# A tuned attention and expert block: value products in blocks of three score chunks, maximum pairs regrouped around them

## What is computed

```python
scores = jnp.einsum('bhqd,bhkd->bhqk', q, k) / jnp.sqrt(jnp.float32(Hd))
attn = jax.nn.softmax(scores, axis=-1)
out = jnp.einsum('bhqk,bhkd->bhqd', attn, v)
out = out.transpose(0, 2, 1, 3).reshape(B, T, D)
return out @ W_o + b_o
...
x = x + ga * attention(layernorm(x) * (1 + ca) + sa)
x = x + gb * experts(layernorm(x) * (1 + cb) + sb)   # 8 experts, 512 tokens each
```

## Time and profile before

| | |
|---|---|
| time, three runs | 1883.09, 1888.33, 1890.05 us; median 1888.33 us |
| time of the profiled execution | 1883.24 us |
| span of the profiled execution | 1881.4 us |
| PE busy | 1737.8 us (92%) |
| DVE busy | 1530.9 us (81%) |
| ACT busy | 1222.2 us (65%) |

### The profile page before, as it was taken

One profiled execution on the slowest core, in us unless ns is written; L12 is line 12 of the kernel. 1 busy time (PEld: TensorE's weight loads), 2 busy tenths in 40 slices (PEclk: granted clock), 3 DMA queues, 4 the chain that ended last, 5 costly groups with the idle time before them and its releaser, 6 DMA issues. The chain is left out here.

```text
span 1881.4 us, 36937 instructions
## 1 busy us (share of the span) xinstructions
PE 1737.8 (92%) x14142; PEld 778.3 (41%) x14142; DVE 1530.9 (81%) x1942; ACT 1222.2 (65%) x2266; POOL 244.7 (13%) x301
## 2 busy tenths in 40 slices
PE   5986999999999999999999999999999861599997
PEld 3652333333333333333333333333333650265665
DVE  4437999999999999999999999999995578544431
ACT  1331888888888888888888888888888210112121
POOL 2004002200010000001000000000000361242422
PEclk8995999999999999999999999999999965699999
DMA  5444243223232223222223222223200530043432
GB/s 180 178 186 61 43 95 70 36 37 57 43 61 39 36 42 57 39 47 53 36 46 54 39 36 51 49 46 53 37 12 16 173 123 0 23 98 103 108 93 23
DMA packets 87458, 121.32 MB, mean 64 GB/s; under 512 B 22592, under 2 KB 65152, under 8 KB 84096
## 3 DMA queue, kind: packets, MB, share of 16 engines
q1 hardware_dynamic: 78880, 109.12, 25.9%
q0 software_dynamic: 6144, 8.39, 2.7%
q10 hardware_dynamic: 2272, 1.61, 0.3%
HBM read 80.53 MB, written 38.54 MB: 63 GB/s over the span
## 5 line engine op out<-in xcount | busy, mean ns | idle before, releaser
L696 DVE TENSOR_REDUCE pmax<-ps 128x2 f32<-128x1024 f32 x1024 | 1230.2, 1220 | 46.1 <-PE ps L725 35.8
L678 ACT ACTIVATE pt<-ps 128x512 f32<-128x512 f32 x2048 | 1111.4, 597 | 204.4 <-PE ps L738 164.8
L725 PE MATMUL ps<-kp,qp 48*128 48x512 f32 x2048 | 734.1, 460 | 23.8 <-DMA kp<-k_parts 15.4
L738 PE MATMUL ps<-qp,kp 50*128 50x512 f32 x2048 | 752.0, 446 | 0.0
L750 PE MATMUL ps<-pt,v_st 128*32 128x256 f32 x8192 | 656.3, 392 | 0.0
L738 PEld LDWEIGHTS ps<-qp,kp 50*128 50x128 f32 x2048 | 315.0, 186 | 409.5 <-ACT pt L678 350.4
L725 PEld LDWEIGHTS ps<-kp,qp 48*128 48x128 f32 x2048 | 289.8, 188 | 63.3 <-issue 25.5
L750 PEld LDWEIGHTS ps<-pt,v_st 128*32 128x32 f32 x8192 | 161.4, 108 | 367.3 <-ACT pt L678 299.7
L1250 ACT ACTIVATE ao<-ps,b_col 128x512 f32<-128x512 f32 x64 | 44.0, 687 | 192.0 <-PE ps L1374 192.0
L619 POOL CAST m_parts<-rowmax_t 128x32 fp32r<-128x32 f32 x64 | 13.5, 211 | 858.0 <-DVE rowmax_t L708 858.0
L1374 PE MATMUL ps<-stage_b,v_all 128*128 128x512 f32 x256 | 118.7, 611 | 1.5 <-DVE stage_b L1266 1.5
(11 more groups left out here) (185 smaller groups left out, 810.3 us busy)
## 6 DMA issues: line engine op xcount, KB each, us to landing
kp<-k_parts SPq DMA_DIRECT2D x192, 128.0 KB, 4.5
v_all<-L_ffn_w SPq DMA_DIRECT2D x16, 1024.0 KB, 8.3
qp<-q_parts SPq DMA_DIRECT2D x192, 64.0 KB, 4.1
q_parts<-pt SPq DMA_DIRECT2D x16, 512.0 KB, 2.7
k_parts<-pt SPq DMA_DIRECT2D x16, 512.0 KB, 3.0
o_rows<-o_sb SPq DMA_DIRECT2D x64, 128.0 KB, 2.0
ao<-L_attn_x SPq DMA_DIRECT2D x2, 2048.0 KB, 18.3
m_rows<-m_parts SPq DMA_DIRECT2D x256, 2.0 KB
```

Of the source, the lines that this page charges most:

```text
L678: nc.scalar.activation(pt[:, s % PTS, half * CH:(half + 1) * CH], bank(n % SCORE_BANKS), ACT.Exp, scale=SCALE).then_inc(scores_out, 1)
L696: v.reduce_max(pmax[:, u % 2, 2 * k:2 * k + 2], group_slot(n).rearrange("p (f t) -> p f t", f=2), AX.X).then_inc(groups_out, 1)
L725: last = mm(group_slot(n)[:, half * CH:(half + 1) * CH], qp[rows, r, a * P:(a + 1) * P], kp[rows, r, c * CH:(c + 1) * CH], start=True, sto ...
L738: mm(bank(n % SCORE_BANKS), kp[rows, h % NBUF, kt * P:(kt + 1) * P], qp[rows, h % NBUF, f * CH:(f + 1) * CH], start=True, stop=True).then_ ...
```

## The change

Values are weighed in **blocks** of three chunks instead of steps of two. A unit of 32 chunks has 11 blocks (`BLOCKS`): a short first one of two chunks and ten of three. A block of three chunks holds a whole step (four products of 256 columns) and half a step (four products of 128 columns). The layout of `acc` is changed so that a half step's columns lie together, and with it the loads of `ao` (two DMAs instead of one for a unit) and of the sums (eight instead of four).

On TensorE, each block is: the value product of the block before the last one, then the scores of three chunks with pairs of maxima around them. In blocks 0, 3, 5, 7 and 9 of a unit there are two pairs, one ahead of the scores and one behind them. In the other blocks of three there is one, behind the first score. In block 2, which has two scores, it comes ahead of them. ScalarE waits for its `pt` slot before each chunk, and copies the sums before chunk 3 of a unit instead of chunk 4.

```diff
 QT = TH // P
 LEAD = 8
 AHEAD = KT + LEAD
-LAG = 3
+BLOCK = 3
+DELAY = 2
+UNIT_CHUNKS = 2 * KT
+BLOCKS = -(-UNIT_CHUNKS // BLOCK)
+FIRST_BLOCK = UNIT_CHUNKS - (BLOCKS - 1) * BLOCK
+QB = CH // 4
 PTS = 6
 HG = D // HD // KD
 BITS = 7
...
 
             acc = bank(7)[:, 0:STRIP]
 
+            def blocks_until(n):
+                u, c = divmod(n, UNIT_CHUNKS)
+                return u * BLOCKS + (c - FIRST_BLOCK) // BLOCK + 2
+
+            def chunks_of(block):
+                u, b = divmod(block, BLOCKS)
+                end = u * UNIT_CHUNKS + FIRST_BLOCK + b * BLOCK
+                return range(end - (BLOCK if b else FIRST_BLOCK), end)
+
             def group_slot(n):
                 return bank(3 + 2 * (n % 2), 2)
 
...
                 def load_output(u):
                     g, f = divmod(u, HALVES)
                     rows = slice((g % HG) * HD, (g % HG + 1) * HD)
-                    cols = slice(f * TH, (f + 1) * TH)
                     strips = o_dram[u].rearrange("(j r) c -> r j c", r=32)
                     sp.wait_ge(o_stored[u % 2], (u // 2 + 1) * 16)
-                    sp.dma_start(ao[rows, g // HG, cols].rearrange("r (j c) -> r j c", c=STRIP),
-                                 strips[0:HD]).then_inc(o_in[f], 16)
+                    for half in range(2):
+                        part = ao[rows, g // HG, f * TH + half * CH:f * TH + (half + 1) * CH]
+                        sp.dma_start(part.rearrange("r (j c) -> r j c", c=QB),
+                                     strips[0:HD, :, half * QB:(half + 1) * QB]).then_inc(o_in[f], 16)
                     if g >= HG:
                         sp.wait_ge(inverse_saved, ((g // HG - 1) * HALVES + f + 1) * 16)
                     for j in range(4):
-                        at = (g % HG) * HD + 4 * j
-                        sp.dma_start(sums_c[at:at + 4, f, :],
-                                     strips[HD, j].rearrange("(q c) -> q c", q=4)).then_inc(sums_in[f], 16)
+                        for half in range(2):
+                            at = (g % HG) * HD + half * (HD // 2) + 2 * j
+                            sp.dma_start(sums_c[at:at + 2, f, :],
+                                         strips[HD, j, half * QB:(half + 1) * QB].rearrange("(q c) -> q c", q=2)
+                                         ).then_inc(sums_in[f], 16)
 
                 def finish_group(u):
                     h, f = divmod(u, HALVES)
...
                                           v_all[:, (h // H) * KT:(h // H + 1) * KT, (h % H) * HD:(h % H + 1) * HD]).then_inc(v_staged, 1)
 
                 def restage_v(h):
-                    pool.wait_ge(pv_done, (h - NBUF + 1) * HALVES * KT)
+                    pool.wait_ge(pv_done, (h - NBUF + 1) * HALVES * BLOCKS)
                     stage_v(h, h % NBUF)
 
                 g = nc.gpsimd
...
                     g.tensor_tensor(low, rowmax_t[:], high, ALU.subtract).then_inc(parts_made, 1)
 
                 def normalise_part(k, f):
-                    pool.wait_ge(o_in[f], (k + 1) * HG * 16)
+                    pool.wait_ge(o_in[f], (k + 1) * HG * 32)
                     pool.wait_ge(inverse_in[f], (k + 1) * HG * 16)
                     normalise(g, k, f).then_inc(normalised, 1)
 
...
             @block.scalar
             def _(act):
                 def take_output(u):
-                    act.wait_ge(pv_done, (u + 1) * KT)
+                    act.wait_ge(pv_done, (u + 1) * BLOCKS)
                     if u > 1:
                         act.wait_ge(o_stored[u % 2], (u // 2) * 16)
                     nc.scalar.copy(o_sb[:, u % 2, :], acc).then_inc(acc_out, 1)
 
-                for s in range(STEPS):
-                    if s % KT == LAG - 1 and s > KT:
-                        take_output(s // KT - 1)
+                for n in range(STEPS * 2):
+                    if n % UNIT_CHUNKS == BLOCK and n > UNIT_CHUNKS:
+                        take_output(n // UNIT_CHUNKS - 1)
+                    s, half = divmod(n, 2)
                     if s >= PTS:
-                        act.wait_ge(pv_done, s - PTS + 1)
-                    for half in range(2):
-                        n = s * 2 + half
-                        act.wait_ge(scores_full, n + 1)
-                        nc.scalar.activation(pt[:, s % PTS, half * CH:(half + 1) * CH], bank(n % SCORE_BANKS),
-                                             ACT.Exp, scale=SCALE).then_inc(scores_out, 1)
+                        act.wait_ge(pv_done, blocks_until(n - 2 * PTS))
+                    act.wait_ge(scores_full, n + 1)
+                    nc.scalar.activation(pt[:, s % PTS, half * CH:(half + 1) * CH], bank(n % SCORE_BANKS),
+                                         ACT.Exp, scale=SCALE).then_inc(scores_out, 1)
                 take_output(UNITS - 1)
 
             @block.vector
...
                 v = nc.vector
                 def invert(u):
                     h, f = divmod(u, HALVES)
-                    dve.wait_ge(sums_in[f], (h + 1) * 64)
+                    dve.wait_ge(sums_in[f], (h + 1) * 128)
                     inverse(v, f).then_inc(inverse_made, 1)
 
                 for n in range(STEPS):
...
                                   kp[rows, r, c * CH:(c + 1) * CH], start=True, stop=True)
                     last.then_inc(groups_full, 1)
 
-                def scores(s, half):
+                def scores(n):
+                    s, half = divmod(n, 2)
                     u, kt = divmod(s, KT)
                     h, f = divmod(u, HALVES)
-                    n = s * 2 + half
                     if kt == 0 and half == 0:
                         pe.wait_ge(maxima_in[u % 2], (u // 2 + 1) * 32)
                     if n >= SCORE_BANKS:
...
                     mm(bank(n % SCORE_BANKS), kp[rows, h % NBUF, kt * P:(kt + 1) * P],
                        qp[rows, h % NBUF, f * CH:(f + 1) * CH], start=True, stop=True).then_inc(scores_full, 1)
 
-                def weigh(s):
-                    u, kt = divmod(s, KT)
+                def weigh(block):
+                    u, b = divmod(block, BLOCKS)
                     h = u // HALVES
-                    if kt == 0:
+                    if b == 0:
                         pe.wait_ge(v_staged, h + 1)
                         if u > 0:
                             pe.wait_ge(acc_out, u)
-                    pe.wait_ge(scores_out, (s + 1) * 2)
-                    for j in range(4):
-                        last = mm(acc[32 * j:32 * (j + 1), :], v_st[:, h % NBUF, kt, :],
-                                  pt[:, s % PTS, j * STRIP:(j + 1) * STRIP], start=kt == 0, stop=kt == KT - 1)
+                    ready = chunks_of(block)
+                    pe.wait_ge(scores_out, ready[-1] + 1)
+                    for s in sorted({n // 2 for n in ready}):
+                        kt = s % KT
+                        halves = [n % 2 for n in ready if n // 2 == s]
+                        first, many = halves[0], len(halves)
+                        probs = pt[:, s % PTS, first * CH:(first + many) * CH].rearrange("p (h t) -> p h t", h=many)
+                        for j in range(4):
+                            last = mm(acc[32 * j:32 * (j + 1), first * QB:(first + many) * QB], v_st[:, h % NBUF, kt, :],
+                                      probs[:, :, j * QB:(j + 1) * QB], start=kt == 0, stop=kt == KT - 1)
                     last.then_inc(pv_done, 1)
 
                 for n in range(AHEAD):
                     fill_group(n)
-                for s in range(STEPS):
-                    first = (s - LAG) % KT == 0
-                    if s >= LAG and not first:
-                        weigh(s - LAG)
-                    scores(s, 0)
-                    if s >= LAG and first:
-                        weigh(s - LAG)
-                    if AHEAD + s < STEPS:
-                        fill_group(AHEAD + s)
-                    scores(s, 1)
-                for s in range(STEPS - LAG, STEPS):
-                    weigh(s)
+                blocks = UNITS * BLOCKS
+                group, chunk = AHEAD, 0
+                for block in range(blocks):
+                    if block >= DELAY:
+                        weigh(block - DELAY)
+                    b = block % BLOCKS
+                    many = FIRST_BLOCK if b == DELAY else BLOCK
+                    twice = b != DELAY and (b == 0 or b > DELAY and b % 2 == 1)
+                    for n in range(many):
+                        if n == (0 if twice or b == DELAY else 1) and group < STEPS:
+                            fill_group(group)
+                            group += 1
+                        scores(chunk)
+                        chunk += 1
+                    if twice and group < STEPS:
+                        fill_group(group)
+                        group += 1
+                for block in range(blocks - DELAY, blocks):
+                    weigh(block)
 
 
         h2_t = pt[:, 1:4:2, :].rearrange("p s (k t) -> p s k t", k=KD)
...
```

(4 more changed lines are left out.)

## The result

The changed kernel took 1916.25 us (median of four runs, 1915.64 to 1930.32), the kernel before 1889.19 (1883.09 to 1917.38). The ratio of the mean times, without the old kernel's slow execution of 1917.38 us, is 1.017, with a 95% interval of 1.011 to 1.024: slower, where 1864 us and faster was forecast. The time lies outside the range.

A forecast was written before the change was run, and what follows sets the result against it. TensorE was taken as the bound, VectorE waiting for it. 61 units at 0.42 us saved give 25.6 us, less 1.7 at the stage's end: 24 off, so 1864 us against 1888.3; range 1840 to 1902.

The forecast's parts named there:

- Value product of three chunks, 0.785 us: On TensorE, 0.57 us for one step plus 0.215 us for two passes of 128 columns; upper bound 1.00 us.
- Rivals 2 and 3: Short 128-column passes don't hide their loads: 1881 us, chance 0.17; or cost much more than half: 1917 us, chance 0.15.
- Length by the fuller half of the rows: TensorE's row-split phases last by products on the fuller half: two 0.67, three 0.91, four 1.15 us.
- TensorE's own sum: TensorE's phases without waits: 3.63 us for two blocks against 3.72 before, 19.39 us a unit.
- The chain of score banks: Third score waits for ScalarE to free one of three banks: two blocks take 3.69 us, not 3.63.
- rival 1: The chain of banks does not bind, so TensorE's 19.39 us a unit holds: 1847 us, chance 0.20.
- Unit 19.67 us: Steady attention unit: 19.39 + 4 x 0.06 + 0.04 us, 0.42 less than 20.09.
- Two waits for each exponential (rival 4): ScalarE's waits break its overlap by 0.06 us each: a unit 20.1 to 20.2 us, about 1893 us, chance 0.08.
- Copy of the sums hidden: The copy ends 0.2 us ahead of the value product that needs it, so 0.25 us a unit goes.
- VectorE costs nothing: Two slots are enough for uneven groups, each read 0.2 us or more before its fill; no cost.
- SP's longer end, 1.7 us: Five more transfers a unit on SP, uncovered only at the stage's end: next stage starts 1.7 us later.
- What it comes to at full clock: 61 units x 0.42 us less 1.7 us, 24 us off 1883.2: 1859 us for a profiled run.

The follow-up runs named there:

- half_exp_burst: `burst_after` with exponentials of 256 columns instead of 512, the left-out half of each chunk standing as 1.0; 1843.93 us in one run, 19.46 us a unit.
- lead9_burst: Changed kernel with a lead of 25 groups instead of 24 before the first step, and 40 dense products ahead of it; 1855.79 us, ratio 0.984.
- layout_only: Changed kernel's accumulator layout, DMAs and waits, with blocks of two chunks in the old order; 1889.54 us, ratio 1.001 to the kernel before.
- burst_after: Changed kernel plus 40 dense bf16 products between the lead of groups and the first step; 1860.81 us, ratio 0.987 to the kernel before.
- spread_burst: Changed kernel, without a burst, with two pairs placed behind the first and second score; 1890.1 and 1944.9 to 1947.6 us, 20.22 us a unit.
- lead7_after: Changed kernel with the first step one group earlier (lead of 23 groups instead of 24), no dense products; median 1870.0 us, ratio 0.990.
- lead9_after: Changed kernel with the first step one group later (lead of 25 groups instead of 24); median 1867.7 us, ratio 0.984 leaving out four of ten executions.
- burst_before: Kernel before plus 40 dense products between the lead of groups and the first step; 1883.68 us, ratio 0.998 to the kernel before.

## Why the prediction was wrong

The step that failed is in the sum: "The first two units, with a lower clock, and the last 24 steps, where ScalarE paces both orders, I leave alone (within 3 us)." The low clock cost 53 us, not 3, and it turned a gain into a loss. I had seen in the earlier trace rows that the clock was low ahead of the stage and full in it, and took the moment of its rise as given. It depends on the stage's first work, and I changed just that. No rival held it. Every rival was about the steady stage, where the mechanism was right and the size nearly so.

Step by step:

- *Value product of three chunks, 0.785 us*: 0.79. A float32 pass of 128 columns costs half of one of 256. Rivals 2 and 3 fall, and the Trainium skill's rule that the prediction cites, that loads hide only behind another row group, does not hold for these passes either (TensorE: Matmul & The Clock Gate, Part 3, The mechanism): two more rounds of passes cost 0.22 us with their loads, half of the 0.43 us of two with 256 columns.
- *Length by the fuller half of the rows*: right. Where nothing holds them (`half_exp_burst`), the phases take 0.66, 0.88 to 0.90 and 1.13 or 1.14 us, counted 0.67, 0.91 and 1.15. TensorE's own sum is then some 19.2 us (the estimate above), counted 19.39.
- *The chain of score banks*: right as a mechanism, and rival 1 falls: loads of the third score are held by ScalarE, and half exponentials take 0.25 us off a unit. The size, put at 0.28, was too small: from the 19.2 us to the 19.61 of `lead9_burst`, where VectorE holds nothing, are some 0.4 us (an estimate).
- *Unit 19.67 us*: 19.71, and the gain of a unit 0.38 instead of 0.42. That it is so close is partly luck: TensorE's sum was counted too long, the bank holds and VectorE too short.
- *Two waits for each exponential (rival 4)*: no cost, by `layout_only`. The rival's price was also added wrongly: with 0.12 us more in each two blocks the terms of the prediction give about 20.3 us a unit and some 1901 us, not 20.1 to 20.2 and 1893.
- *Copy of the sums hidden*: right. It ends 0.22 us ahead of the value product's load, where 0.2 was forecast.
- *VectorE costs nothing*: wrong by 0.10 us a unit. I had counted each slot as free by 0.2 us, but one phase of a unit is held for it (9.3 us of waits in 800). `lead9_burst`, without that hold, has the shorter unit.
- *SP's longer end, 1.7 us*: 1.5. The eight sums DMAs take 2.35 us of SP, not twice the 1.33 of four.
- *What it comes to at full clock*: forecast 1859 us for a profiled run. The changed kernel's fastest execution, without the long low stretch by its time and its mean clock (0.949, as before), took 1857.4, and `burst_after` 1860.8.

Why the changed order leaves the low clock so late is only half settled. Shown is that with a lead of 24 groups the three-chunk blocks bring it (`layout_only` against the change), that the place of the pairs doesn't matter for it (`spread_burst`), that the lead does (`lead7_after`, `lead9_after`), and that dense work ahead cured it in four executions of four. At the low clock both orders keep TensorE occupied and take nearly the same time for a unit: 34.43 us, and by the old kernel's value product to value product at 185.37 and 187.53 us, 2.16 us a step, 34.6 (an estimate from this one step). So it is not that one does clearly more in the same time. What is left is how each repeats, every step or every three, against whatever the chip looks at; that is an inference, and nothing here tests it.

The rows of the old kernel's last low steps, and the first after the rise:

```profile
185.37 0.20 PEld L750 LDWEIGHTS ps<-pt,v_st 128*32 128x32 f32 x8 [0.65 <-issue]
...
187.53 0.20 PEld L750 LDWEIGHTS ps<-pt,v_st 128*32 128x32 f32 x8 [0.65 <-issue]
...
189.70 0.20 PEld L750 LDWEIGHTS ps<-pt,v_st 128*32 128x32 f32 x8 [0.65 <-issue]
...
191.39 0.16 PEld L750 LDWEIGHTS ps<-pt,v_st 128*32 128x32 f32 x8 [0.37 <-issue]
```

## What to carry to other kernels

Where a stage begins at the low clock, ask of every change of its TensorE order what ends the low stretch, and price it at both levels: here 14.7 us for each unit that it lasts. A TensorE that the profile shows as wholly occupied is no sign that the clock will rise, or that it will stay up; 6.3 us of dense work just ahead of the stage bought 55 here. Phases in different splits of the array can be priced from starts, entry and drain apart from the passes, and then the banks and slots behind them must be walked through for the new order, all of them: the one I left out undid my own improvement.

## What the runs showed of the hardware

- With TensorE shown busy from end to end, the clock stayed at 1.2 GHz for some 140 us (180 to 322 and 321 us) in both profiles of one program; the times of eight of its ten executions fit this.
- With TensorE as busy, a full clock fell back for some 20 us (`burst_before`, 186 to 206 us).
- A lead of one group (1.1 us) less or more moved the rise from 322 us to some 251 us (0.71 of full in the window to 260) or just before 220 us, in one profile each.
- Row-split phases of two, three and four products on the fuller half of the rows: 0.66, 0.89 and 1.13 us where nothing holds them (`half_exp_burst`), 0.23 to 0.24 us for each more product; two column-split float32 passes of 128 columns, 0.22 us together (0.79 against 0.57 us), loads included.
